# Attention over small graphs with a residual and a layer norm: the work of each engine ordered in halves of a graph

## The reference, cut to what matters

```python
q, k, v = (proj(Wq, bq), proj(Wk, bk), proj(Wv, bv))        # x @ W.T + bias, split in 8 heads
scores = jnp.einsum('bhqd,bhkd->bhqk', q, k) * SCALE        # SCALE = 32 ** -0.5
mask = (adj_matrix + bond_matrix)[:, None, :, :]            # both are adj: 2 * adj
attn = jax.nn.softmax(scores * mask, axis=-1)
ctx = jnp.einsum('bhqk,bhkd->bhqd', attn, v)                # heads put side by side again
x = _layernorm(x + ctx @ Wo.T + bo)                         # eps 1e-5, over the features
```

## Time and profile before

| | |
|---|---|
| median of 3 runs | 583.24 us (579.94 to 585.08) |
| the profiled execution, own time | 583.36 us |
| its span in the trace | 581.6 us |
| PE busy | 439.7 us (76%) |
| DVE busy | 417.6 us (72%) |
| ACT busy | 371.0 us (64%) |
| POOL busy | 247.1 us (42%) |
| mean granted clock of PE | 0.89 of full speed |
| DMA | 94.14 MB, mean 162 GB/s |

### The profile page before, as it was taken

The page is one execution under the profiler, slowest core; times in us unless marked ns, Lnnn a source line. Parts: engine busy times, 40 slices in busy tenths (PEclk is TensorE's granted clock), DMA queues, the critical chain, the costliest instruction groups (busy, mean ns, idle before and its releaser), DMA issues.

```text
span 581.6 us, 12230 instructions
## 1 busy us (share of the span) xinstructions
PE 439.7 (76%) x3604; PEld 318.9 (55%) x3604; DVE 417.6 (72%) x1717; ACT 371.0 (64%) x1222; POOL 247.1 (42%) x379
## 2 busy tenths in 40 slices
PE   8777779777778777778767679767778877776665
PEld 7545556555556555556555456555556655554444
DVE  5756687677686686786777677786787777677874
ACT  4775666675676666766666666675676676676650
POOL 3215234354361642635445352643544364232354
PEclk9988898888899788998799888897998888899877
DMA  6664565665755757566565746766575574754661
GB/s 236 181 159 149 118 176 164 163 183 133 233 122 147 189 141 212 129 176 167 140 192 139 225 120 167 200 158 188 132 191 155 131 199 106 212 130 107 173 165 65
DMA packets 60004, 94.14 MB, mean 162 GB/s; under 512 B 7969, under 2 KB 49186, under 8 KB 59938
## 3 DMA queue, kind: packets, MB, share of 16 engines
q1 hardware_dynamic: 46610, 68.19, 47.4%
q10 hardware_dynamic: 13328, 25.17, 12.7%
HBM read 26.22 MB, written 8.39 MB: 60 GB/s over the span
## 4 chain that ended last, share of the span: by engine, by line
PE 37%; DVE 33%; issue 13%; ACT 13%; ACTq 1%; DMA 1%; POOL 1%; SPq 0%; DVEq 0%; POOLq 0%
DVE probs L453 19%; PE row_bank L243 16%; PE ctx_bank L351 10%; ACT probs L636 7%; PE proj_bank L290 6%; DVE boxes L471 6%; DVE context L486 3%; PE turn_bank L260 3%; ACT kq L657 3%; DVE low_top L462 3%; ACT inverse L650 3%; DVE mean_var L504 1%; DMA w_whole<-in_wv 1%; ACTq L629 1%; DVE top L453 1%
## 5 line engine op out<-in xcount | busy, mean ns | idle before, releaser
L636 ACT ACTIVATE probs<-probs,low_top 128x256 f32<-128x256 f32 x512 | 255.4, 501 | 186.8 <-DVE low_top L462 186.8
L453 DVE CUSTOM_DVE_ANT_0 probs<-row_bank,adj_rows 128x256 f32<-128x256 f32 x512 | 192.8, 413 | 137.8 <-PE row_bank L243 137.4
L290 PE MATMUL proj_bank<-xt_parts,w_parts 128*128 128x512 f32 x360 | 128.8, 486 | 85.3 <-ACT kq L657 85.3
L290 PEld LDWEIGHTS proj_bank<-xt_parts,w_parts 128*128 128x128 f32 x360 | 71.4, 221 | 128.4 <-ACT kq L657 91.3
L471 DVE STREAM_TRANSPOSE boxes<-probs 128x512 f32<-128x512 f32 x192 | 135.2, 705 | 0.0
L243 PE MATMUL row_bank<-kq 32*128 32x256 f32 x1024 | 94.0, 492 | 12.5 <-DVE top L453 12.3
L769 POOL CAST ctx_parts<-context 128x512 fp32r<-128x512 f32 x31 | 18.9, 609 | 186.5 <-DVE context L486 186.5
L636 ACT ACTIVATION_READ_ACCUMULATOR probs<-probs,low_top 128x1 f32 x512 | 96.7, 189 | 0.0
L243 PEld LDWEIGHTS row_bank<-kq 32*128 32x128 f32 x1024 | 56.6, 224 | 43.4 <-issue 39.2
L260 PE MATMUL turn_bank<-ident,probs 128*128 128x128 f32 x256 | 40.3, 281 | 33.6 <-ACT inverse L650 33.6
L351 PE MATMUL ctx_bank<-carried,v_boxed 128*32 128x256 f32 x760 | 63.6, 398 | 0.0
(11 more groups left out here) (74 smaller groups left out, 485.0 us busy)
## 6 DMA issues: line engine op xcount, KB each, us to landing
carried<-boxes SPq DMA_DIRECT2D x256, 192.0 KB, 3.8
adj_rows<-in_adj ACTq DMA_DIRECT2D x16, 512.0 KB, 3.5
v_boxed<-v SPq DMA_DIRECT2D x128, 64.0 KB, 2.2
xr<-in_x ACTq DMA_DIRECT2D x16, 512.0 KB, 6.1
out<-result ACTq DMA_DIRECT2D x31, 256.0 KB, 2.2
xt<-in_x_t SPq DMA_DIRECT2D x15, 512.0 KB, 3.7
xt<-in_x_t SPq DMA_DIRECT2D x2, 256.0 KB, 3.3
w_whole<-in_wk ACTq DMA_DIRECT2D x2, 128.0 KB, 3.5
```

The source lines that it names most:

```text
L290: last = nc.tensor.matmul(proj_bank[:], w_parts[:, a, which, t, c * P:(c + 1) * P], xt_parts[:, pair % 2, b, t, :], start=(half_ == 0 and ...
L453: last = nc.vector.tensor_tensor_reduce(probs[:, h % RING, t * S:(t + 1) * S], row_bank[j][:, t * S:(t + 1) * S], adj_rows[:, (g // 2) % 2 ...
L636: last = nc.scalar.activation(tile, tile, ACT.Exp, bias=low_top[:, g % 2, J * c + j, t:t + 1], accum_out=sums[:, g % 2, t, j * T + c:j * T ...
```

## The change

PE does whole pieces: `rows`, then a whole K or Q, in each half of the step. `weigh_v` moves from the end of step `g + 1` to step `g + 2`, behind its first K or Q. DVE masks the four heads of a group in one go, with `lower_top` one head behind, and turns the three heads of a group in one `STREAM_TRANSPOSE` of 128 x 1536 elements; the rest of its work stands between the groups. `row_stats` comes a step earlier, and `divide(g)` at the end of step `g` instead of in step `g + 1`. ACT reads a K or Q behind the fourth head of a group. The semaphore `boxed` counts groups instead of heads.

```diff
@@ SP, carry_boxes(n)
-                sp.wait_ge(boxed, BOXED * (n + 1))
+                sp.wait_ge(boxed, n + 1)
@@ PE, step(g)
                 if is_pair(ahead):
                     for half_ in range(2):
                         project_kq(ahead, 2 * (g % 2), half_)
+                if is_graph(g - 2):
+                    weigh_v(g - 2)
                 if is_group(2 * g - 1):
                     turn_probs(2 * g - 1)
                 if is_graph(g + 1):
                     project_v(g + 1)
-                if is_pair(ahead):
-                    project_kq(ahead, 2 * (g % 2) + 1, 0)
                 if is_graph(g):
                     rows(2 * g + 1)
                 if is_pair(ahead):
-                    project_kq(ahead, 2 * (g % 2) + 1, 1)
+                    for half_ in range(2):
+                        project_kq(ahead, 2 * (g % 2) + 1, half_)
                 if is_graph(g - 1):
                     turn_shares(g - 1)
                 if 0 <= g - 2 < LAST:
                     project_out(g - 2)
                 if is_group(2 * g):
                     turn_probs(2 * g)
-                if is_graph(g - 1):
-                    weigh_v(g - 1)
@@ DVE, reduce_rows(n, j)
-                    wait(dve, boxed, BOXED * (n - RING // J) + j + 1)
+                    wait(dve, boxed, n - RING // J + 1)
@@ DVE, box
-            def box(n, j):
-                dve.wait_ge(probs_ready, J * n + j + 1)
-                if j == 0:
-                    wait(dve, carried_in[n % 2], 64 * (n // 2))
-                nc.vector.transpose(boxes[:, n % 2, :, j, :].rearrange("p a (f q) -> p f a q", q=D),
-                                    probs[:, (J * n + j) % RING, :].rearrange("p (f a k) -> p f a k", a=J, k=D)
+            def box(n):
+                dve.wait_ge(probs_ready, J * n + BOXED)
+                wait(dve, carried_in[n % 2], 64 * (n // 2))
+                first = J * n % RING
+                nc.vector.transpose(boxes[:, n % 2].rearrange("p a h (f q) -> p (h f) a q", q=D),
+                                    probs[:, first:first + BOXED, :].rearrange("p h (f a k) -> p (h f) a k", a=J, k=D)
                                     ).then_inc(boxed, 1)
@@ DVE, step(g)
-                for s in range(H):
-                    n, j = 2 * g + s // J, s % J
-                    if is_group(n):
-                        reduce_rows(n, j)
-                        lower_top(n, j)
-                    behind = H * g + s - LAG
-                    if is_group(behind // J) and behind % J < BOXED:
-                        box(behind // J, behind % J)
...
+            def mask_group(n):
+                for j in range(J):
+                    reduce_rows(n, j)
+                    if j > 0:
+                        lower_top(n, j - 1)
+                lower_top(n, J - 1)
...
+                if is_group(2 * g):
+                    mask_group(2 * g)
...
+                if 0 <= g - 2 < LAST:
+                    scale_context(g - 2)
+                if is_group(2 * g - 1):
+                    box(2 * g - 1)
+                if 0 <= g - 3 < LAST:
+                    aggregate(g - 3)
+                if is_group(2 * g + 1):
+                    mask_group(2 * g + 1)
+                if 0 <= g - 2 < LAST:
+                    add_residual(g - 2)
+                if is_group(2 * g):
+                    box(2 * g)
+                if 0 <= g - 2 < LAST:
+                    for t in range(T):
+                        row_stats(g - 2, t)
+                if is_graph(g):
+                    divide(g)
@@ ACT, step(g)
-                    if s == 1 and g == 0:
+                    if s == 0 and g == 0:
                         copy_v(0)
+                        read_kq(1, 0)
...
-                    if s == 2 and is_pair(ahead):
-                        read_kq(ahead, 2 * (g % 2))
-                    if s == 2 and is_group(2 * g - 1):
+                    if s == 1 and is_group(2 * g - 1):
                         move_turned(2 * g - 1)
...
                     if s == 3 and is_graph(g + 1):
                         copy_v(g + 1)
-                    if s == 5 and is_graph(g - 1):
+                    if s == 3 and is_pair(ahead):
+                        read_kq(ahead, 2 * (g % 2) + 1)
+                    if s == 3 and is_graph(g - 1):
                         copy_inverse(g - 1)
-                    if s == 5 and is_pair(ahead):
-                        read_kq(ahead, 2 * (g % 2) + 1)
-                    if s == 7 and is_group(2 * g):
+                    if s == 5 and is_group(2 * g):
                         move_turned(2 * g)
+                    if s == 7 and is_pair((g + 1) // 2 + 1):
+                        read_kq((g + 1) // 2 + 1, 2 * ((g + 1) % 2))
@@ POOL, step(g): spread_shares(g - 1) moves from s == 3 to s == 0, cut_context(g - 2) from s == 1 to s == 3
```

More of the change, by code:

```diff
@@ L33 @@
 BOXED = J - 1
-LAG = 3
 LAST = B - 1
@@ L580, in _ @@
                 read_first_q(c)
-            def step(g):
-                for s in range(H):
-                    n, j = 2 * g + s // J, s % J
-                    if is_group(n):
-                        reduce_rows(n, j)
-                        lower_top(n, j)
-                    behind = H * g + s - LAG
-                    if is_group(behind // J) and behind % J < BOXED:
-                        box(behind // J, behind % J)
-                    if g == 0 and s == 2:
-                        low_weights(3)
-                    if g == 0 and s == 3:
-                        dve.wait_ge(bias_made, 1)
-                        nc.vector.tensor_copy(bias[:], ctx_bank[:, 0:E]).then_inc(bias_ready, 1)
-                    if s == 1 and 0 <= g - 2 < LAST:
-                        scale_context(g - 2)
-                    if s == 2 and is_graph(g - 1):
-                        divide(g - 1)
-                    if s == 3 and 0 <= g - 3 < LAST:
-                        for t in range(T):
-                            row_stats(g - 3, t)
-                    if s == 4 and 0 <= g - 3 < LAST:
-                        aggregate(g - 3)
-                    if s == 7 and 0 <= g - 2 < LAST:
-                        add_residual(g - 2)
@@ new lines, in mask_group @@
+            def mask_group(n):
[4 more added lines that the diff above has]
+                lower_top(n, J - 1)
+            def step(g):
+                if is_group(2 * g):
+                    mask_group(2 * g)
+                if g == 0:
+                    low_weights(3)
+                    dve.wait_ge(bias_made, 1)
+                    nc.vector.tensor_copy(bias[:], ctx_bank[:, 0:E]).then_inc(bias_ready, 1)
+                if 0 <= g - 2 < LAST:
[15 more added lines that the diff above has]
+                    divide(g)
@@ L819, in step @@
                 for s in range(H):
-                    if s == 0 and g % 2 == 1 and is_pair(g // 2 + 2):
+                    if s == 0 and is_graph(g - 1):
+                        spread_shares(g - 1)
+                    if s == 1 and g % 2 == 1 and is_pair(g // 2 + 2):
                         cut_x(g // 2 + 2, 1)
-                    if s == 1 and 0 <= g - 2 < LAST:
+                    if s == 3 and 0 <= g - 2 < LAST:
                         cut_context(g - 2)
-                    if s == 3 and is_graph(g - 1):
-                        spread_shares(g - 1)
                     if s == 4 and is_graph(g - 1):
```

## The result

The changed kernel takes 444.44 us (median of 4 runs, 439.89 to 446.21) against 583.58 us before (583.24 in the table, of one execution fewer); the ratio is 0.761, 95% interval 0.754 to 0.768. The forecast was 436 us, 424 to 475. The profiled execution has a span of 443.2 us and an own time of 445.0.

What follows compares the result with a forecast made beforehand. The bound was a ring of mask, exponentials, reading, half projection and scores, 17.24 us a graph. Cut, ACT and DVE's 12.25 plus 0.25 gives 12.5; 12.7 + 31 x 12.5 + 34.3 = 434.5, plus 1.8: 436 us, range 424 to 475.

Steps and rivals of the forecast that it cites:

- The old ring: Mask of three heads, exponentials, reading, half a projection, scores, mask: said to bound the 17.24 us graph, cut by the change.
- ACT and DVE's ring: From first mask through ACT's exponentials, copies and one reading to the reciprocal: 12.25 us a graph, the longest ring.
- DVE's sum: DVE's own work per graph after the change: 12.0 us (11.8 to 12.3), from 13.0 occupied before.
- PE's sum: PE's own work per graph at full clock: 11.2 us, with nothing added or removed by the change.
- The reason that I gave for the clock: PE's 3.2 us pause ahead of the slow stretch is gone, so full clock, 2.4 GHz, was counted.
- X: End of the box of group 2g - 1 to its four DMAs' last landing: 5.6 us, up to about 7 without cost.
- The formula: Ring over two graphs through the DMAs: X + 5.4 + 11.9; a graph takes (X + 17.3) / 2 if over 12.25.
- 1 (427 to 455): The forecast itself: 12.2 to 13.1 us a graph, 427 to 455 us; chance 0.66.
- part of 2: Rival of late DMAs, PE waiting ahead of ctx_bank: 13.2 to 14.2 us a graph, 457 to 488 us; chance 0.15.
- rival 3: PE's clock still falls once a graph: PE's sum about 14.9, up to 15.5 us a graph, 488 to 530; chance 0.09.
- rival 4: PE's clock stays low: work takes 1.75 times, about 20 us a graph, about 669 us; chance 0.04.
- 5: An overlooked wait in DVE's strict order keeps the period near 17 us: 560 to 590 us; chance 0.04.

Runs made afterwards that it cites:

- dve_only: The kernel before with DVE's part alone as changed (four masks in a row, one turning a group, divide at the step's end): 557.41 us, ratio 0.952.
- order_only: The changed kernel with DVE's part as before, only scale_context one place later; PE, ACT, POOL as changed: 451.31 us, ratio 0.772.
- read_inside: The changed kernel with ACT reading K and Q behind the third and sixth head, as before the change: 472.69 us, ratio 0.809.
- divide_late: The changed kernel with a graph's reciprocal behind the next graph's first four masks instead of ahead of them: 439.17 us, ratio 0.750.
- early_divide: The changed kernel with adj and x loaded at the end of the step before and the reciprocal behind the next graph's first four masks: 425.32 us, ratio 0.727.
- three_boxes: The changed kernel with the single turning of 128 x 1536 made as three of 128 x 512, one behind the other: 445.70 us, ratio 0.761.
- loads_early: The changed kernel with ACT's loads of adj and x issued at the end of the step before, behind the seventh and eighth head: 447.00 us, ratio 0.765.
- loads_late: The changed kernel with ACT's loads of adj and x moved from behind the second and third head to behind the sixth and seventh: 481.66 us, ratio 0.832.

## Why the prediction was right, point by point

- **The old ring and its cutting**: right. `dve_only` keeps it and stays at 557 us; `order_only` cuts it and gets 451. How much of the cut is PE's order and how much that of ACT and POOL is only known for the readings (28 us, `read_inside`).
- **ACT and DVE's ring, 12.25 us**: 12.23 in the undisturbed graphs. Its parts too: the first exponential starts 217.80 - 216.25 = 1.55 us behind the first mask (1.6 said), ACT's eight heads, four copies and one reading take 228.19 - 217.80 = 10.39 (10.34 said), and 0.29 are left for the signal and the reciprocal (0.3 said). That `divide_late` and `early_divide`, which cut it, have graphs of 11.64 us shows that it was the bound.
- **DVE's sum, 12.0 us**: 0.36 too high; 11.88 busy (rows that overlap by a few hundredths), and 11.64 as a period in `early_divide`. Nothing hung on it, since the ring was longer. Four masks take 219.34 - 216.25 = 3.09 us (3.2 said), a box 221.64 - 219.95 = 1.69 (1.75 said), against 3 x 0.63 in the earlier trace rows and 1.81 for three in a row in `three_boxes`; so 0.06 to 0.1 us of a turning is fixed. The Trainium skill ("VectorE: DVE Perf Modes", on the TRN2 errata) says that such an operation pays a fixed latency once per instruction; the trace agrees in kind.
- **PE's sum, 11.2 us**: 11.12 busy in the clean graph; and the clock was 1.00 there, 0.975 over the run. The reason that I gave for the clock is weaker than it looks. The pause ahead of the slow stretch of the earlier trace rows is this one:

```profile
331.37 0.92 PEld L290 LDWEIGHTS proj_bank<-xt_parts,w_parts 128*128 128x128 f32 x3 [3.23 <-ACT kq L657]
```

  It is as long as the one of 3.20 us in the earlier trace rows, over which, and behind which, the clock stayed at 1.00. So pauses of this length were followed by either level before, and what decides between them is not shown here.
- **The DMAs**: the term that was mis-sized. I gave 0.25 us a graph for three engines and the DMAs together; from 12.25 to the measured mean it is 0.4 to 0.5. The bound itself held where it could be seen: in the graph shown, the box ended at 221.7, the last of its DMAs landed at 228.2 and PE began `weigh_v` at 228.3; X = 6.4, and nothing was lost. But 6.4 is not the 5.6 of my sum, the median of the 32 graphs is 6.3, so only 0.7 of the 1.4 us of slack was there, and X is not steady: it is over 7 in seven graphs. At the worst place it was 11.5 us. The formula gives 11.5 + 17.3 = 28.8 us for the two graphs from that box; they took 31.6 (17.6 and 14.0 from reciprocal to reciprocal). The chain there, then ACT's queue and DVE's row in order of time:

```profile
293.71 3.16 SPq L187
...
296.96 0.93 SPq L187
...
297.93 2.03 SPq L187
...
300.66 7.20 DMA carried<-boxes
...
307.99 3.64 PE ctx_bank L349 x32
```

```profile
293.16 0.45 ACTq L629 DMA_DIRECT2D adj_rows<-in_adj  x1
...
305.94 1.78 DVE L468 STREAM_TRANSPOSE boxes<-probs 128x1536 f32<-128x1536 f32 x1 [5.19 <-DMA carried<-boxes]
```

  In the terms of my X: the box ended at 296.3, SP was free for its DMAs 0.6 us later (nothing said), the first three issues took 3.7 us (1.85 said), and the last DMA landed 7.2 us behind its issue (3.7 said). The long landing is the largest part; the issue of 3.16 us, of the group before, cost only the 0.6. Just ahead of it ACT's queue had put 1.25 MB in flight (a store at 292.41, adj at 293.16, x at 294.12). Two things were missing in the formula besides. DVE's box waits for the DMAs of the group two before it to have emptied its half of the tile `boxes`, a wait that I had not laid out: the DMA issued at 293.71 landed 12.1 us later, and the box waited 5.19 us for it. So the DMAs of the other group, to which I gave a whole step in the expectation of `loads_early`, have about 7 us from the last one's issue before DVE wants its tile. And PE was idle for 4.88 us ahead of `weigh_v`; the granted clock was 0.50 behind that, and `weigh_v` took 3.64 us instead of 1.9.
- **The ends**: first mask at 13.07 (12.7), then 31 x 12.73, then 35.4 us behind the last graph's first mask (34.3). Of the 8.7 us between the forecast span of 434.5 and 443.2, 7.1 are the period's and 1.5 the ends'.
- **The rivals**: 1 (427 to 455) as the rhythm, with part of 2 on top of it: its sign, PE waiting for DMAs ahead of `ctx_bank`, is there in 25 waits of 30.7 us in all, though in the clean graphs they cost nothing. Nothing of 3 beyond the pauses that late DMAs make, nothing of 4 and 5. Two prices of these rivals were loose: the 14.9 us of rival 3 takes twice the time at half clock, where rival 4 has 1.75 times; and in the 3.04 us of `weigh_v` in the earlier trace rows the mean clock was 0.63, not a half: at 0.50 it took 3.64.

## What to carry to other kernels

Where engines wait for each other in a ring, write each engine's order so that nothing that waits for a late partner stands ahead of what the next partner needs; here the order on PE, ACT and POOL was worth 132 of the 139 us, and DVE's part alone 26; with the readings of K and Q back at their old places 111 were left, so they are not where most of the gain lies. Once the rings are cut, several limits lie close together (11.1, 11.6 and 12.2 us a graph here), and single further edits brought nothing or 2%, two of them together 5%; look at which waits are left together. Bulk loads then have to be placed by the time at which they are in flight beside the urgent transfers, read from the trace and not from the place in the code.

## What the runs showed of the hardware that was not expected

- The same bytes, issued a few us elsewhere in the step, changed the run from 444.5 to 481.7 us. The medians hide it: `carried` lands in 3.8 us in the median before the change, in 4.2 in the changed kernel (at a DMA share of 0.81 over 200 us, against 0.63 before), and in 3.9 in `loads_late`, the slowest of the three placements of the loads. What counts is the last of the four DMAs on which PE waits; the longest landing in the changed kernel was 12.1 us.
- Issuing a DMA of `carried` took SP 0.54 to 3.16 us in the changed kernel, 0.65 in the median. What makes an issue long is not shown.
- A DMA on ACT's queue was issued while activations written ahead of it were still to run: in `loads_early` adj at 216.54 and x at 217.08, 2.2 and 2.6 us ahead of the end of the last exponential that the code puts before them.
